# A new written-out order on all five queues, and a later place for the weights and the second image

## The reference, cut to what matters

```python
x = x + attention(_gn(x), g, w_qkv, mem_kv, w_out, b_out)
x = x + conv(_gn(x), w3, w1, b, 4)
# attention: xn = x / max(norm over channels, 1e-12) * g * sqrt(C)
#   q, k, v = split(w_qkv @ xn); 4 heads of 32; 4 memory columns before k and v
#   q = softmax(q over the head's 32) * 32**-0.5 ; k = softmax(k over pixels)
#   context = k v^T ; out = w_out @ (context^T q) + b_out
# conv: w3 only where (j-i) % 4 == 0, 3x3, padding 1;
#   w1 (1x1) where (j-i) % 4 != 0 ; bias b summed over its inputs
# _gn: groups of 4 channels, (v - mean) / sqrt(var + 1e-5)
```

## Time and profile before

| what | value |
|---|---|
| median of 3 runs | 2093.57 us (2093.47 to 2094.22) |
| the profiled execution | 2094.91 us |
| its span | 2093.1 us |
| TensorE busy | 1958.1 us, 94% |
| VectorE busy | 1736.9 us, 83% |
| ScalarE busy | 1353.9 us, 65% |
| GpSimd busy | 1363.3 us, 65% |
| DMA queue of SP | 308.73 MB, 70.9% of 16 engines |

### The profile page before, as it was taken

One profiled execution on the slowest core, in us unless ns is written; L12 is line 12 of the kernel. 1 busy time (PEld: TensorE's weight loads), 2 busy tenths in 40 slices (PEclk: granted clock), 3 DMA queues, 4 the chain that ended last, 5 costly groups with the idle time before them and its releaser, 6 DMA issues.

```text
span 2093.1 us, 50607 instructions
## 1 busy us (share of the span) xinstructions
PE 1958.1 (94%) x21199; PEld 1044.2 (50%) x21199; DVE 1736.9 (83%) x3144; ACT 1353.9 (65%) x1476; POOL 1363.3 (65%) x737
## 2 busy tenths in 40 slices
PE   2889999999999999999999999999999999999996
PEld 0445545555544555544555544555544555554552
DVE  5688888888988888988888988888988888888863
ACT  2567666767666666666666666676766676766661
POOL 5566667766667676666676667676666676666662
PEclk9799999999999999999999999999999999999997
DMA  4367767887667878667787667778777778766675
GB/s 104 61 130 150 154 145 154 168 166 152 146 151 155 170 157 165 147 142 154 167 156 164 151 149 147 163 160 172 147 146 151 156 166 167 152 147 148 134 142 125
DMA packets 349427, 312.96 MB, mean 150 GB/s; under 512 B 299152, under 2 KB 299920, under 8 KB 341008
## 3 DMA queue, kind: packets, MB, share of 16 engines
q1 hardware_dynamic: 347712, 308.73, 70.9%
q10 hardware_dynamic: 1168, 0.98, 0.2%
q0 software_dynamic: 320, 0.01, 0.0%
HBM read 68.10 MB, written 67.11 MB: 65 GB/s over the span
## 4 chain that ended last, share of the span: by engine, by line
PE 67%; DVE 21%; ACT 4%; POOL 3%; DMA 2%; issue 1%; SPq 1%; ACTq 0%
PE pair_ps L799 15%; PE pair_ps L781 8%; PE pair_ps L762 7%; DVE km L1111 7%; PE pair_ps L705 5%; PE bank_ps L699 5%; PE pair_ps L790 4%; PE pair_ps L742 4%; POOL exp_kT_lo L447 3%; PE bank_ps L772 3%; PE pair_ps L765 3%; DVE nrm L1098 2%; DVE parts L1098 2%; PE bank_ps L751 2%; DVE u L1108 2%; PE bank_ps L754 2%
## 5 line engine op out<-in xcount | busy, mean ns | idle before, releaser
L799 PE MATMUL pair_ps<-replicas,w_rep 96*32 96x512 f16 x8192 | 488.9, 383 | 8.9 <-DMA replicas<-yg_lo 8.9
L444 POOL TENSOR_TENSOR u_lo<-u,u_hi 128x1024 f16<-128x1024 f32 x128 | 270.0, 2146 | 273.9 <-ACT u_hi L551 273.9
L447 POOL TENSOR_TENSOR exp_kT_lo<-exp_kT,exp_kT_hi 128x1024 f16<-128x1024 f32 x128 | 301.0, 2361 | 179.1 <-ACT exp_kT_hi L560 179.0
L450 POOL TENSOR_TENSOR u_lo<-exp_q,u_hi 128x1024 f16<-128x1024 f32 x128 | 272.5, 2140 | 113.2 <-ACT u_hi L566 113.2
L799 PEld LDWEIGHTS pair_ps<-replicas,w_rep 96*32 96x32 f16 x8192 | 206.1, 96 | 275.4 <-issue 89.4
L1163 DVE SCALAR_TENSOR_TENSOR image<-pair_ps,image 128x512 f32<-128x512 f32 x256 | 172.2, 681 | 121.9 <-PE pair_ps L799 118.2
L440 POOL TENSOR_SCALAR u<-image,st 128x1024 f32<-128x1024 f32 x128 | 187.9, 1479 | 110.4 <-DVE st L1062 110.4
L551 ACT ACTIVATE u_hi<-u 128x1024 f16<-128x1024 f32 x128 | 130.8, 1045 | 177.6 <-DVE u L1108 177.5
L566 ACT ACTIVATE u_hi<-exp_q 128x1024 f16<-128x1024 f32 x128 | 135.3, 1057 | 161.1 <-DVE exp_q L1150 161.0
L557 ACT ACTIVATE exp_kT<-pair_ps,zcol 128x1024 f32<-128x1024 f32 x128 | 141.0, 1101 | 144.4 <-PE pair_ps L742 144.3
L536 ACT ACTIVATE exp_kT<-u,zcol 128x1024 f32<-128x1024 f32 x128 | 146.0, 1143 | 93.7 <-POOL u L440 92.4
(11 more groups left out here) (179 smaller groups left out, 4832.1 us busy)
## 6 DMA issues: line engine op xcount, KB each, us to landing
image<-in_x SPq DMA_DIRECT2D x256, 256.0 KB, 4.8
out<-image SPq DMA_DIRECT2D x512, 128.0 KB, 2.2
replicas<-yg_hi SPq DMA_DIRECT2D x256, 165.0 KB, 3.9
replicas<-yg_hi SPq DMA_DIRECT2D x256, 107.2 KB, 5.1
replicas<-yg_lo SPq DMA_DIRECT2D x128, 165.0 KB, 4.3
replicas<-yg_lo SPq DMA_DIRECT2D x128, 107.2 KB, 3.8
uT_hi<-u_hi SPq DMA_TRANSPOSE x128, 3.4
uT_lo<-u_lo SPq DMA_TRANSPOSE x128, 3.4
```

What stands on the lines that cost most here:

```text
L444: pool.tensor_tensor(px(UL, v), px(U, v), px(UH, v), ALU.subtract).then_inc(ul_ready, 1)
L447: pool.tensor_tensor(KL[:, v % 2], KT[:, v % 2], KH[:, v % 2], ALU.subtract).then_inc(kl_ready, 1)
L450: pool.tensor_tensor(px(EL, v), px(EQ, v), px(EH, v), ALU.subtract).then_inc(el_ready, 1)
L799: mm = pe.matmul(conv_ps[32 * r:32 * r + 32, j % 2], w_rep[0:32 * SLOTS, tap, r], rep[:, j * ROWS + dy:(j + 1) * ROWS + dy, dx:dx + SIDE], ...
```

## The change

Nothing is computed otherwise; what changes is the place of the pieces in each engine's order, a few PSUM buffers, and the engines of two pieces of the setup.

- Start: SP asks for image 1 only when image 0 has landed. The weights are permuted on ACT and not on DVE, and no longer ahead of x_seed. The conv weights are split on DVE (also their high half) behind norm_guard of image 0, ahead of norm_parts. GpSimd makes minus_max behind its first step.
- Boundary of the step: normalise 1 to 3, maxima 0 to 2, ring 6 and the broadcasts go from the beginning of the next step to the end of this one.
- TensorE: rough_q(0) ahead of rings; keys 2 and 3 both ahead of context 0; context 2 ahead of queries 3, and the denominators straight behind these; contexts 3 and dense 0 ahead of ring 0; rings 1 and 2 apart, ring 2 beside norm_sums 2 and 3; ring 3 behind mix 0 and 1; mix 2 behind ring 3; mixes now use pairs 0 and 1, and broadcasts 0 to 2 all pair 0.
- DVE, ACT, POOL: accordingly. max_q(0) is ahead of row_k, low_y(1) on POOL behind low_k(2) and group_norm_y(2), high_y(3) on ACT behind den_power and square(0), norm_log ahead of high_q(3).
- SP: turn_u(3) ahead of the replicas, store 1 at the end of the step.

The core of the diff, of TensorE's order and of the start:

```diff
+            load(0, 0)
+            load(0, 1)
+            for h in range(2):
+                sp.wait_ge(x_in[h][0], at_load(0))
+            load(1, 0)
+            load(1, 1)
...
                 if c is not None:
                     replicate_high(c, 0)
+                    sp.wait_ge(lo_odd, at(c, UNITS // 2, 1))
                     sp.wait_ge(lo_even, at(c, UNITS // 2, 1))
                     replicate_low(c, 0)
...
                     group_norm_y(c, 0)
                     group_norm_y(c, 1)
+                if a is not None:
+                    pool.wait_ge(kh_ready, at(a, UNITS, 3))
+                    low_k(a, 2)
+                if c is not None:
+                    group_norm_y(c, 2)
                     low_y(c, 1)
...
+                    keys(a, 2, pair_ps[1])
+                    keys(a, 3, pair_ps[0])
                     context(a, 0, bank_ps[0])
...
+                    queries(a, 1, pair_ps[2])
+                    queries(a, 2, pair_ps[0])
+                    context(a, 2, bank_ps[0])
                     group_means(0, bank_ps[1], x_group)
+                    queries(a, 3, pair_ps[1])
                     denominators(a, 0, bank_ps[1])
...
                     conv_ring(c, 0)
+                    turn_context(bank_ps[1])
                     conv_dense(c, 1)
                     conv_ring(c, 1)
                     den_broadcast(a, 0, pair_ps[0])
...
                     norm_sums(p, 2, bank_ps[1])
                     norm_sums(p, 3, bank_ps[1])
+                    conv_ring(c, 2)
+                    mix(a, 0, pair_ps[0])
+                    mix(a, 1, pair_ps[1])
+                    conv_dense(c, 3)
+                    conv_dense(c, 4)
+                    conv_ring(c, 3)
+                    mix(a, 2, pair_ps[1])
+                    inv_norm(p, 0, pair_ps[0])
+                    conv_ring(c, 4)
+                    inv_norm(p, 1, pair_ps[0])
+                    conv_dense(c, 5)
+                    mix(a, 3, pair_ps[1])
+                    inv_norm(p, 2, pair_ps[0])
                     conv_ring(c, 5)
+                    inv_norm(p, 3, pair_ps[1])
+                    rough_k(p, 0, pair_ps[0])
+                    conv_dense(c, 6)
+                    rough_k(p, 1, pair_ps[1])
+                    rough_k(p, 2, pair_ps[0])
+                    conv_ring(c, 6)
...
+                if first(s):
+                    split_conv_weights()
```

More of the change, by code:

```diff
@@ L492, in step @@
                     low_k(a, 3)
+                if p is not None:
+                    pool.wait_ge(x_stat, at(p, X_STEPS, X_STEPS))
+                    group_norm_x(p, 0)
+                    if c is not None:
+                        pool.wait_ge(lo_odd, at(c, UNITS // 2, 1))
+                    group_norm_x(p, 1)
                 if c is not None:
@@ L498, in step @@
                 if p is not None:
[L499 to L501 removed]
+                    if c is not None:
+                        pool.wait_ge(lo_even, at(c, UNITS // 2, 2))
                     group_norm_x(p, 2)
@@ L639, in step @@
                     square(p, 0)
+                if c is not None:
+                    high_y(c, 3)
+                if p is not None:
                     act.wait_ge(xg_ready, at(p, UNITS, 2))
@@ L670, in step @@
                     square_y(a, 0)
[L672 to L676, removed]
+                    high_q(a, 3)
+                if p is not None:
+                    act.wait_ge(u_ready, at(p, UNITS, 1))
+                    high_u(p, 0)
+                    act.wait_ge(u_ready, at(p, UNITS, 2))
+                    high_u(p, 1)
+                if a is not None:
+                    act.wait_ge(y_ready, at(a, UNITS, 2))
+                    square_y(a, 1)
+                if p is not None:
+                    act.wait_ge(u_ready, at(p, UNITS, 3))
+                    high_u(p, 2)
+                if a is not None:
+                    act.wait_ge(y_ready, at(a, UNITS, 3))
+                    square_y(a, 2)
+                if p is not None:
+                    act.wait_ge(u_ready, at(p, UNITS, 4))
+                    high_u(p, 3)
+            act.wait_ge(weights_in, 16 * WEIGHT_DMAS)
+            act.activation(perm_qkv, raw_qkv.rearrange("p t (i r) -> p t r i", r=RES), ACT.Copy).then_inc(setup_act, 1)
+            act.activation(perm_w1, raw_w1.rearrange("p (i r) -> p r i", r=RES), ACT.Copy).then_inc(setup_act, 1)
+            for t in range(TAPS):
+                last = act.activation(perm_w3[:, t], raw_w3.rearrange("p (i r t) -> p t r i", r=RES, t=TAPS)[:, t], ACT.Copy)
             last.then_inc(setup_act, 1)
@@ L758, in queries @@
             def queries(s, v, ps):
+                if first(s) and v == 0:
+                    pe.wait_ge(const_made, POOL_STEPS)
                 for j in (2 * v, 2 * v + 1):
@@ L917, in step @@
                 if c is not None:
+                    pe.wait_ge(lo_even, at(c, UNITS // 2, 1))
+                    conv_dense(c, 0)
+                if a is not None:
+                    pe.wait_ge(uT_in[3], at(a, 32, 32))
+                    pe.wait_ge(kl_ready, at(a, UNITS, 4))
+                    context(a, 3, bank_ps[0])
+                if c is not None:
                     pe.wait_ge(lo_in[0], at(c, 16 * RES, 16 * RES))
@@ L1219, in step @@
                     rows_q(a, bank_ps[1])
+                if p is not None and not first(p):
+                    x_stats(p, 1)
                 if c is not None:
@@ L1286, in step @@
                     norm_parts(p, 1)
+                if c is not None:
+                    dve.wait_ge(conv_done, at(c, CHUNKS, 4))
+                    finish(c, 3)
+                if p is not None:
+                    dve.wait_ge(inv_bcast, at(p, UNITS, 1))
+                    normalise(p, 0, pair_ps[0])
+                if a is not None:
+                    dve.wait_ge(mixed, at(a, UNITS, 3))
+                    residual(a, 2, pair_ps[1])
+                if p is not None:
+                    dve.wait_ge(inv_bcast, at(p, UNITS, 2))
+                    normalise(p, 1, pair_ps[0])
                 if c is not None:
```

421 lines of the change are left out of this document (178 added, 243 removed).

## The result

The change made the kernel slower, by 0.3%, where a gain of 0.7% was forecast: 2099.77 us (median of 7 runs, 2099.01 to 2104.47) against 2093.74 of the kernel before, measured beside it; ratio 1.0032 [1.0021, 1.0044]. Forecast were 2079 us and "faster" with 0.70. The profiled execution took 2099.77, its span is 2098.0, 4.9 longer than that of before.

A forecast was written before the change was run, and what follows sets the result against it. TensorE was taken as the bound. Steady images -10, start -5.0 and second image +0.5 gave -14.5 us, from 2094.91 to 2080.4; the median, 1.3 lower, was forecast at 2079 us, range 2040 to 2110.

The forecast's parts named there:

- two parts steps with a brush against low_q(3): VectorE's chain after residual 1, from 4.0 to 6.6 us behind mix(a,0); the chain's TensorE waits: -0.62 an image.
- Low keys -0.34: TensorE's wait for GpSimd's low keys, hidden by two key units ahead of context 0: -0.34 us an image.
- denominators' parts -0.46: TensorE's wait for the denominators' parts, covered by ring 0, turning, dense 1 and ring 1: -0.46 us an image.
- Denominators +0.46: Denominators straight behind query 3, their second half waiting for its exponentials: +0.46 us an image, bounds 0.1 and 1.5.
- Eleventh block +0.22: Eleven blocks of 32 columns an image on TensorE, before ten; one more drain round trip: +0.22 us an image.
- Replicas +0.40 at every image: Ring 0 comes up at 24.1, the last band 0 replica lands at 24.5: +0.4 us, bounds 0 and 2.5.
- Rival B: Ring 0 waits for the low replicas, 0.9 us or more an image; kernel slower, 2112 or 2142 us; chance 0.19.
- The sum of an image: All terms of one steady image together: -0.34 us, times 30 images -10 us.
- Start -5.0: First image: weights at about 16, broadcast at 38.0, 9.4 us earlier, of which 4.4 is given back.
- What is given back behind it: Behind the first broadcast: broadcasts 1 and 2, rough k3 and the row wait for VectorE: +4.4 us.
- Image 1 +0.5: The second image, alone on TensorE, has the same lengthening without cover: +0.5 us.
- End 0: After the last mix both orders wait for the same statistics, low part and replicas: 0 us.

The follow-up runs named there:

- e1: The changed kernel with GpSimd's low_q(3) made to wait until VectorE has written the parts of the norm: 2063.26 us, ratio 0.9849 to the kernel before.
- e4: The changed kernel with context 2 moved behind queries 3, so between them and the denominators: 2119.79 us, ratio 1.0116 to the kernel before.
- e7: e6 with GpSimd's group_norm_y(3) made to wait for VectorE's parts of the denominators: 2053.15 us, ratio 0.9806 to the kernel before.
- e3: The changed kernel with GpSimd's low_y(1) again ahead of low_k(2) and group_norm_y(2): 2107.17 us, ratio 1.0058 to the kernel before.
- e2: The changed kernel with GpSimd's minus_max made behind the first image's last low_u: 2100.88 us, ratio 1.0030 to the kernel before.
- e6: e1 with e4, so low_q(3) behind the norm's parts and context 2 behind queries 3: 2081.65 us, ratio 0.9938 to the kernel before.
- e8: e1 with SP's turn_u(3) moved between the high and low replicas of band 0: 2063.67 us, ratio 0.9855 to the kernel before.
- e10: e1 with one extra GpSimd instruction of low_q's form and size set off by the first parts step: 2098.28 us, ratio 1.0024 to the kernel before.
- e11: e1 with one extra GpSimd instruction of low_q's form and size placed behind low_q(3): 2062.43 us, ratio 0.9848 to the kernel before.

## Why the prediction was wrong, step by step

**The failed step** is in VectorE's chain: "two parts steps with a brush against low_q(3)", priced at 0.2 (from 4.0 to 6.6, less the 2.4 of two steps alone). The two steps took 4.12 us (1103.54 to 1107.66), 2.38 in e1 where they are undisturbed: 1.74 late. Some of it ends in idle times of VectorE that were forecast behind it (0.6 at the first broadcast), so keys(p,0) comes 25.12 behind mix(a,0) and not 24.1. With the meeting taken away (e1) it is 24.0: the rest of that chain was right, and the waits before rough k1, rough k2 and keys 0 nearly so (0.38, 0.71 and 0.2 from start to start, for 0.33, 0.7 and 0.4). The rows to price it were there: the 1.57 for 0.75 at 1089.77 in the earlier trace rows was read as a surcharge of working beside GpSimd, when it is the rest of a GpSimd instruction that VectorE has to sit out. POOL in the kernel before:

```profile
1089.38 1.43 POOL L440 TENSOR_SCALAR u<-image,st 128x1024 f32<-128x1024 f32 x1
```

This instruction ends at 1090.81, VectorE's 0.53 behind it, at 1091.34. For one that begins just behind the start of a low_q this is up to 2 us, and low_q(3) had been moved into exactly this place, since high_q(3) waits behind two more pieces on ScalarE. At 30 images the 1.0 is 31 us, more than the whole forecast gain: without it the kernel is some 30 us faster than before, as e1 is.

**Low keys -0.34, denominators' parts -0.46**: both waits gone, as forecast; e4 shows that the cover of the second is thin. **Denominators +0.46**: nearly right, at 0.40 (the terms that are written there give 0.44). PE and ACT in the changed kernel:

```profile
1081.92 2.33 PE L780 MATMUL bank_ps<-exp_q,red_head 128*32 128x512 f32 x16
...
1082.03 1.12 ACT L571 ACTIVATE exp_q<-pair_ps,zcol 128x1024 f32<-128x1024 f32 x1 [1.23 <-PE pair_ps L773]
```

The last exponentials start after the denominators have, and end 1.23 into them. From start to start they hold TensorE for 2.26, and 1.86 when covered (e4); the cover is worth 0.40 an image (e1 to e7). **Eleventh block +0.22**: rings still hold 1.86 and the dense product ahead of them 0.32, as in the rows; it was not tried by itself.

**Replicas +0.40 at every image**: wrong. Low_y(1) ends 17.55 behind keys 0 (forecast 18.0); "SP is idle there" was wrong, SP is still issuing the high replicas:

```profile
1075.14 5.65 SPq L320 DMA_DIRECT2D replicas<-yg_hi  x8
1080.89 2.44 SPq L326 DMA_DIRECT2D replicas<-yg_lo  x4
...
1086.30 1.93 PE L807 MATMUL pair_ps<-replicas,w_rep 96*32 96x512 f16 x32
```

Ring 0 starts 23.9 behind keys 0 (forecast 24.1) and waits for nothing. In 6 of 30 images it waits, 3.8 us in all. In one of these SP's list is behind:

```profile
384.11 5.04 SPq L333 DMA_TRANSPOSE uT_lo<-u_lo  x1
389.19 5.05 SPq L320 DMA_DIRECT2D replicas<-yg_hi  x8
394.35 3.45 SPq L326 DMA_DIRECT2D replicas<-yg_lo  x4
...
399.50 1.93 PE L807 MATMUL pair_ps<-replicas,w_rep 96*32 96x512 f16 x32 [0.30 <-DMA replicas<-yg_lo]
```

The last turning ahead of the replicas takes 5.04 and not 3.35 or 3.80, as in two images without a wait. Rival B (ring 0 waits for the low replicas, 0.9 or more at each image) had the right sign of the result for a wrong reason: e3 took most of its wait away and the kernel got slower. That 2099.77 lies inside the range of 2040 to 2110 is luck too, since the upper end was drawn for B.

**The sum of an image**: forecast 62.01, undisturbed 62.27. The chain is 1.0 longer; from keys 0 to mix(a,0) it is 37.15 where 62.01 - 24.1 = 37.9 were forecast, so 0.76 shorter: 0.40 of it is the replicas' wait that was not there, 0.36 is left without a name. The longer images add 5 us over 30 that no term had. The six images with a late replica are longer by 5.7 of the 8.3 in all, image 2 by 1.6 (1.3 before); why SP's transposes are slow in some images stays open.

**Start -5.0**: it was -0.6. The weights landed 2.5 later than the sum by bandwidth said; "GpSimd's minus_max is hidden" looked only at who needs minus_max, not at whom it disturbs: 2.95 (e2). Together 5.4, against the 5.2 by which the broadcast was late. What is given back behind it was forecast at 4.4 and is 3.6 (from 4.2 earlier at the broadcast to 0.6 earlier at the turn). **Image 1 +0.5**: it was +2.9. With low_q(3) behind the parts it takes 62.0 in e1, but from 61.5 (e6) to 64.3 (e8) in the other runs that hold low_q(3) back; what it varies with isn't settled. **End 0**: it was -0.2.

The forecast did say, under rival B, that every such meeting of the new order pays again, but it counted only low_k against low_y. Other meetings in the new order were not looked for; a list of them would have held the parts steps.

## What to carry to other kernels

Before an order is changed, list VectorE's casts and two-input instructions on SBUF that the bound waits for, and lay GpSimd's instructions over them: each meeting costs what is left of the other's instruction, not a share. If one falls there, let GpSimd wait for VectorE (36 us here), and do so before other edits are judged, since one that gains 0.4 an image can lose 1.2 by shifting the next meeting (e4, e6, e7).

## What the runs showed of the hardware

In these runs VectorE's casts f32 to bf16 or f16 in SBUF and its instructions with two SBUF inputs, when they begin while a GpSimd instruction runs, stand still until that one ends. Those of the parts and of the first weights end 0.14 to 0.55 behind it: 2.63 for 0.29 beside a memset, 4.85 for 0.43 beside a selection, 2.40 for 0.43 and 2.50 for 0.75 beside a subtraction. The one that begins first is not held. Where the cast at 1104.78 takes its 0.43, GpSimd's subtraction, begun in the same 0.01 us, takes 2.41 for 2.13; in e10 the cast begins 0.01 behind GpSimd's and takes 2.40, and GpSimd's its 2.13. It goes both ways in the earlier trace rows: of the 3.09 of VectorE's low_y 1.08 lie behind the end of GpSimd's low_y(1) (1072.70), and of the 3.10 of GpSimd's low_k 2.0 behind the end of VectorE's (1073.78). Not held are those that read PSUM with one SBUF input (1.28 in e11), and the statistics of x, which have one f32 input in SBUF; the whole run of the changed kernel has no slow one among 256, though 251 of them begin while GpSimd runs:

```profile
L1041 DVE BATCH_NORM_STATS2 bn<-image x256: 672/677/698, 9.7 to 1954.2; 128x6 f32<-128x512 f32 x128
```

The Trainium skill (SBUF — State Buffer, Who interferes with whom) states an exclusive lock on a pair of ports that GpSimd and VectorE share: a VectorE instruction in a 2-port mode contends with GpSimd, one with two SBUF inputs with a GpSimd instruction that reads SBUF, and the one that comes first has the pair for its whole length. The rows agree; that the casts run in such a mode no run here shows.
